# Wider warming, a new load order, and GpSimd's and VectorE's setup work reordered in a kernel of 16 conditioned tiles

## The reference

```python
x = x + einsum('bct,bcd->bdt', x, W0[cond])          # W0: 16 x 32 x 32
base  = einsum('bsi,oi->bso', x, W)                  # W: 512 x 512
low   = einsum('bsi,bir->bsr', x, A[label])          # A: 5 x 512 x 32
delta = einsum('bsr,or->bso', low, Bw) * 0.5         # Bw: 512 x 32
x = x + base + delta
```

## Time and profile before

| | us |
|---|---|
| median of 3 runs | 88.79 |
| lowest, highest | 87.93, 89.1 |
| the profiled execution | 88.51 |
| its span (first to last instruction) | 86.7 |
| TensorE busy in it | 82.6 |
| VectorE, ScalarE, GpSimd busy | 55.8, 39.6, 23.3 |

### The profile page before, as it was taken

One profiled execution on the slowest core, in us unless ns is written; L12 is line 12 of the kernel. 1 busy time (PEld: TensorE's weight loads), 2 busy tenths in 40 slices (PEclk: granted clock), 3 DMA queues, 4 the chain that ended last, 5 costly groups with the idle time before them and its releaser, 6 DMA issues.

```text
span 86.7 us, 1411 instructions
## 1 busy us (share of the span) xinstructions
PE 82.6 (95%) x463; PEld 72.9 (84%) x463; DVE 55.8 (64%) x117; ACT 39.6 (46%) x80; POOL 23.3 (27%) x37
## 2 busy tenths in 40 slices
PE   5999999999999999999999999999999999999950
PEld 5999999998888988898889888988898888889940
DVE  3672879975984696469744984499249933731550
ACT  0544492233547573457255616551754273415440
POOL 5322798977008001800170008000710000000000
PEclk9999999999999999999999999999999999999999
DMA  1999990370000494646037502770250015000606
GB/s 27 314 350 310 199 188 19 83 178 12 8 0 8 147 267 81 203 126 176 2 140 230 134 0 83 230 186 0 80 177 0 0 50 192 8 0 3 239 14 228
DMA packets 12393, 10.16 MB, mean 117 GB/s; under 512 B 1508, under 2 KB 9572, under 8 KB 12388
## 3 DMA queue, kind: packets, MB, share of 16 engines
q1 hardware_dynamic: 11444, 9.24, 38.1%
q10 hardware_dynamic: 432, 0.59, 2.1%
q0 software_dynamic: 512, 0.26, 1.7%
HBM read 5.90 MB, written 4.19 MB: 116 GB/s over the span
## 4 chain that ended last, share of the span: by engine, by line
PE 95%; DVE 1%; issue 0%
PE p_u L588 15%; PE p_u L589 15%; PE p_u L590 15%; PE p_low L573 5%; PE p_low L578 5%; PE p_low L574 4%; PE p_low L639 4%; PE p_u L599 4%; PE p_y L605 4%; PE p_y L606 4%; PE p_y L608 4%; PE p_u L616 3%; PE p_y L588 2%; PE p_y L589 2%; PE p_y L590 2%; PE p_y L643 2%
## 5 line engine op out<-in xcount | busy, mean ns | idle before, releaser
L252 POOL DMA_INDIRECT w_sel<-in_L_cond_weights,w_row x16 | 16.3, 1019 | 33.4 <-DVE diag L499 30.3
L588 PE MATMUL p_u<-m_hi,xt_hi 128*128 128x512 f32 (+1 forms) x60 | 22.6, 377 | 0.0
L589 PE MATMUL p_u<-m_lo,xt_hi 128*128 128x512 f32 (+1 forms) x60 | 22.6, 377 | 0.0
L590 PE MATMUL p_u<-m_hi,xt_lo 128*128 128x512 f32 (+1 forms) x60 | 22.5, 375 | 0.0
L410 DVE TENSOR_TENSOR xt_lo<-xt,xt_hi 128x512 fp32r<-128x512 f32 x14 | 10.1, 728 | 8.4 <-ACT xt_hi L308 8.4
L396 DVE STREAM_TRANSPOSE xt<-x_sb 128x512 f32<-128x512 f32 x14 | 15.1, 1091 | 0.0
L416 DVE TENSOR_TENSOR u_lo<-p_u,u_hi 128x512 fp32r<-128x512 f32 (+1 forms) x15 | 9.3, 652 | 8.9 <-ACT u_hi L313 8.8
L318 ACT ACTIVATE y_sb<-p_y 128x512 f32 (+1 forms) x13 | 7.7, 591 | 12.2 <-PE p_y L608 12.2
L590 PEld LDWEIGHTS p_u<-m_hi,xt_lo 128*128 128x128 f32 x60 | 11.3, 188 | 2.1
L588 PEld LDWEIGHTS p_u<-m_hi,xt_hi 128*128 128x128 f32 x60 | 11.3, 188 | 1.9
L589 PEld LDWEIGHTS p_u<-m_lo,xt_hi 128*128 128x128 f32 x60 | 11.3, 188 | 1.8
(11 more groups left out here) (92 smaller groups left out, 126.7 us busy)
## 6 DMA issues: line engine op xcount, KB each, us to landing
x_sb<-in_x SPq DMA_DIRECT2D x28, 128.0 KB
out<-y_sb SPq DMA_DIRECT2D x7, 512.0 KB, 3.2
w_sb<-in_L_cond_W ACTq DMA_DIRECT2D x2, 256.0 KB, 3.9
w_sb<-in_L_cond_W SPq DMA_DIRECT2D x2, 256.0 KB, 3.8
x_rows<-in_x SPq DMA_DIRECT2D x2, 256.0 KB, 4.5
out<-y_sb SPq DMA_DIRECT2D x2, 256.0 KB, 2.1
a_sb<-in_L_cond_lora_A SPq DMA_DIRECT2D x1, 256.0 KB, 5.3
w_sel<-in_L_cond_weights,w_row POOLq DMA_INDIRECT x16
```

The costliest lines, as they stand in the source:

```text
L252: nc.gpsimd.indirect_dma_start(out=w0_sel[:, t, :], out_offset=None, in_=W0_rows, in_offset=bass.IndirectOffsetOnAxis(ap=w0_row[:, t:t + 1 ...
L588: mm(to, xt_hi[:, slot, c, rows], m_hi[:, c, cols], start=(c == 0 and half != 1), stop=False)
L589: mm(to, xt_hi[:, slot, c, rows], m_lo[:, c, cols], start=False, stop=False)
L590: mm(to, xt_lo[:, slot, c, rows], m_hi[:, c, cols], start=False, stop=False)
```

## The change

- The warming becomes 6 fp32r products with 512 columns (the same 128 columns read four times) instead of 7 fp32 products with 128.
- SyncE loads x tile 0 right behind Bw, and then all four W tiles in the order of their use (1, 0, 3, 2). ScalarE loads A's part of label 0 and the ids.
- The ids are converted by GpSimd, after its identities and before its adds on W, instead of by VectorE. TensorE transposes x tile 0 and spreads the ids ahead of all W tiles.
- VectorE makes `fold_parts` and `fold_to` between the diagonals of W tiles 1 and 0, and splits x tile 0 as before the split of M.
- TensorE transposes x tile 1 ahead of `lora_half(1)`.
- GpSimd makes `ad_lo` ahead of the first two gathers. ScalarE and VectorE handle `kept` of the first pair ahead of its `diag`.

```diff
--- before.py
+++ after.py
@@ -45,7 +45,7 @@
     ROWS = 2 * P
-    WARM = 7
+    WARM = 6
     H = O // 2
...
@@ -72,7 +72,7 @@
 
-        warm = sb("warm", [P, P])
+        warm = sb("warm", [P, P], F32R)
         ident = sb("ident", [P, P])
...
@@ -199,11 +199,9 @@
             sp.dma_start(bw_sb[:], Bw.rearrange("(o p) r -> p o r", p=P)).then_inc(s_bw_in, 16)
-            sp.dma_start(w_sb[:, 0], W[0:P, :]).then_inc(s_w_in[0], 16)
             sp.dma_start(x_rows[:, 0], x_tile[0]).then_inc(s_rows_in[0], 16)
-            sp.dma_start(ids_i[:, 0], cond.unsqueeze(0)).then_inc(s_cond_in, 16)
-            sp.dma_start(ids_i[:, 1], label.unsqueeze(0)).then_inc(s_label_in, 16)
-            sp.dma_start(w_sb[:, 2], W[2 * P:3 * P, :]).then_inc(s_w_in[2], 16)
+            for o in W_ORDER:
+                sp.dma_start(w_sb[:, o], W[P * o:P * (o + 1), :]).then_inc(s_w_in[o], 16)
             sp.dma_start(x_rows[:, 1], x_tile[1]).then_inc(s_rows_in[1], 16)
...
@@ -242,6 +240,10 @@
 
+            pool.wait_ge(s_cond_in, 16)
+            pool.wait_ge(s_label_in, 16)
+            nc.gpsimd.tensor_copy(ids_r[:], ids_i[:]).then_inc(s_ids, 1)
+
             for o in W_ORDER[2:]:
...
@@ -276,13 +278,12 @@
                                     ALU.subtract).then_inc(s_adiff, 1)
+            pool.wait_ge(s_adiff, 1)
+            pool.wait_ge(s_adhi, 1)
+            nc.gpsimd.tensor_tensor(ad_lo[:], a_diff[:], ad_hi[:].bitcast(F32), ALU.subtract).then_inc(s_adlo, 1)
             pool.wait_ge(s_w0_row, BT)
...
             gather(1)
-
-            pool.wait_ge(s_adiff, 1)
-            pool.wait_ge(s_adhi, 1)
-            nc.gpsimd.tensor_tensor(ad_lo[:], a_diff[:], ad_hi[:].bitcast(F32), ALU.subtract).then_inc(s_adlo, 1)
 
...
@@ -293,8 +294,8 @@
             act.dma_start(a_sb[:, 0].rearrange("p c r -> p (c r)"), A_cols[:, 0]).then_inc(s_a0_in, 16)
-            act.dma_start(w_sb[:, 1], W[P:2 * P, :]).then_inc(s_w_in[1], 16)
-            act.dma_start(w_sb[:, 3], W[3 * P:4 * P, :]).then_inc(s_w_in[3], 16)
+            act.dma_start(ids_i[:, 0], cond.unsqueeze(0)).then_inc(s_cond_in, 16)
+            act.dma_start(ids_i[:, 1], label.unsqueeze(0)).then_inc(s_label_in, 16)
 
...
@@ -350,8 +351,8 @@
             split_x(3, 1, 1)
+            hi_kept(0)
             hi_diag(0, 0)
-            hi_kept(0)
             stack_low(0)
...
@@ -431,7 +432,7 @@
 
-            nc.vector.memset(warm[:], 1.0).then_inc(s_warm, 1)
+            nc.vector.memset(warm[:].bitcast(F32), 1.0).then_inc(s_warm, 1)
             for j in range(BT):
...
@@ -442,7 +443,7 @@
                                            ALU.add).then_inc(s_row_of, 1)
-            nc.vector.tensor_copy(ones_r[:], warm[0:1, :]).then_inc(s_ids, 1)
+            nc.vector.tensor_copy(ones_r[:], warm[0:1, :].bitcast(F32)).then_inc(s_ids, 1)
 
...
@@ -457,24 +458,25 @@
 
-            dve.wait_ge(s_pool, 3)
-            for o in W_ORDER[:2]:
+            def diag_w(k):
+
+                o = W_ORDER[k]
                 dve.wait_ge(s_w_in[o], 16)
...
 
+            dve.wait_ge(s_pool, 3)
+            diag_w(0)
             dve.wait_ge(s_pool, 4 + Q)
...
             nc.vector.tensor_copy(fold_to[:], fold_parts[:]).then_inc(s_group, 1)
-
-            dve.wait_ge(s_cond_in, 16)
-            dve.wait_ge(s_label_in, 16)
-            nc.vector.tensor_copy(ids_r[:], ids_i[:]).then_inc(s_ids, 1)
+            diag_w(1)
             dve.wait_ge(s_ids_all, 1)
             nc.vector.tensor_copy(ids_all[:].rearrange("p u b -> p (u b)"), p_fold[:, 0:2 * B]).then_inc(s_ids_sb, 1)
+            split_rows(0, p_low)
 
...
@@ -483,7 +485,6 @@
 
-            split_rows(0, p_low)
             split_m(0, 0)
...
@@ -511,10 +512,10 @@
             split_x(3, 1, 1)
-            spread(0, 0, used=1)
             dve.wait_ge(s_keep, 1)
...
             split_low(0)
+            spread(0, 0, used=1)
             split_diag(0, 0)
...
@@ -636,7 +637,7 @@
             for i in range(WARM):
-                mm(p_low[:, 0:P], warm[:], warm[:], start=True, stop=True)
+                mm(p_low[:], warm[:], warm[:].unsqueeze(1).broadcast_to([P, 4, P]), start=True, stop=True)
 
...
@@ -655,12 +656,12 @@
             transpose_groups(p_y[1], a_rep).then_inc(s_aT, 1)
+            transpose_rows(0, p_low)
+            spread_ids()
             pe.wait_ge(s_diag, 1)
...
             transpose_w(1)
-            transpose_rows(0, p_low)
-            spread_ids()
             pe.wait_ge(s_b_stack, 1)
...
@@ -668,9 +669,9 @@
             transpose_w(3)
-            lora_half(1)
             pe.wait_ge(s_ids_sb, 1)
             transpose_rows(1, p_fold)
+            lora_half(1)
 
...
             main_tile(p_y[0], 0, 0, left, half=0)
```

## The result

The changed kernel takes 89.23 us (median of 20 runs, 88.51 to 89.83), the kernel before 88.50 (20 runs, 87.93 to 89.1). The ratio is 1.0084, 95% interval 1.0057 to 1.0111: slower by 0.8%, where 0.8 us faster was forecast. The profiled execution took 89.68 us with a span of 87.9, against 88.51 and 86.7.

The account below looks back on a forecast made before the run. TensorE, busy 95% of the span, was taken to bound the kernel; gains could come only from the first 20 us. Waits of -0.67 and warming of -0.05 made -0.7 us: 87.8 or 88.1, called 88.0, range 87.0 to 89.2.

Parts of the forecast that it names:

- GpSimd reordered: `ad_lo` before the gathers: removes TensorE's waits of 0.19 us at `ad_lo` and 0.23 at `low_pair(1)`; later gathers stay covered.
- the worst bound: Gathers landing by 18.9 us, at most 2.4 after GpSimd's second; work ends at 21.8, second fold wants it at 22.4.
- The third rival: Waits only change their name: W0 or W2 late, or gathers holding VectorE; gives back 0.5 to 0.8 us, 88.7; chance 0.16.
- The loop and the tail: TensorE has no idle time there, 8.98 us per pair of tiles, so the change can't shorten them.
- The waits at tile 1, at `ad_lo` and at `low_pair(1)`: TensorE's excess of 0.25, 0.19 and 0.23 us at these places goes, 0.67 us in sum.
- The ids on GpSimd: GpSimd converts the ids at about 4 to 5 us, taking 0.4 to 1 us; nothing waits.
- The landings: First loads by sum of bytes: x tile 0 at 3.9 us, W1 4.7, W0 5.5, W3 6.3, W2 7.0, x tile 1 7.8.
- spare time for W0: W0's transfer and diagonal add have 1.4 us before TensorE needs them, so the load order costs nothing.
- The warming: Six wide products at the start: clock effect taken as 0, bounded by -1.0 and +2.8 us; at most 0.05 us gained otherwise.
- The later clock: Rival: TensorE's full clock comes later in the setup; 89.5 us, or 90.8 by the bound; chance 0.14.
- the hole: TensorE does nothing for about 0.35 us, from 3.65 to 4.0, between the warming and the first transposes.

Follow-up runs that it names:

- e3_load_held: The changed kernel, with SyncE issuing x of pair 3 only when gathers 0 and 1 have landed: six runs from 87.32 to 91.25 us, median 90.15.
- e7_adlo_between: The changed kernel, with GpSimd's order made gather 0, `ad_lo`, gather 1: 88.12 us, ratio 0.9946 to the kernel before.
- e2_gather_first: The changed kernel, with the first two gathers back ahead of `ad_lo` on GpSimd: 88.35 us, ratio 0.9977 to the kernel before.
- e10_no_gather_wait: The changed kernel, with pair 0's mix leaving out the rows of W0 and the wait for gathers 0 and 1: 87.26 us, ratio 0.9863.
- e6_two_queues: The changed kernel, with W tiles 1 and 3 on ScalarE's queue behind the ids, 0 and 2 on SyncE's: 89.59 us, ratio 1.0115.
- e5_adlo_first_only: The kernel before, with only `ad_lo` moved ahead of gathers 0 and 1 on GpSimd: 92.52 us, median of six.
- e4_wide_warm_only: The kernel before, with only the wide warming of 6 fp32r products of 512 columns: 88.34 us, ratio 0.9966.

## Why the prediction was wrong

**The step that failed** is the price of "GpSimd reordered": "with that bound they land by 18.9 ... Covered by 0.6 us at the worst bound". Mix ran at 20.20 instead of 18.9, 1.3 us later, and even 18.9 would have been too late. So two terms were too small and a deadline was missing.

- Issue: gather 1 was put at 15.5 to 16.5 and ran 16.11 to 17.50. The W tiles landed late (W2's add ended at 8.71 instead of 7.6), so `w_row`, `a_diff` and `ad_lo` were each 0.5 us or more behind my times, and the gather took 1.39 us on GpSimd instead of the 0.95 of the earlier trace rows. This is 1.0 of the 1.3 us.
- Flight: I took 2.4 us from the end of the gather to its use as an upper bound for any place. It came from a stretch in which no other load ran. The gather's new place lies beside x of pair 3, a load that SyncE issues when pair 1's x is transposed. It took 2.70 us there, and 1.57 in e3_load_held, where that load was held back. This is the other 0.3 us: the bound was loose for a quiet stretch, and a bound read from a quiet stretch is none for a busy one.
- The work behind mix was priced right: up to the end of `kept_lo` it took 2.83 us (2.9 forecast). TensorE wanted the second fold at 22.2 (22.4 forecast), so with mix at 20.20 it waited 0.9.
- Deadline: I followed the delay to the second fold and stopped. The stricter deadline was the low products of pair 2. They end a chain from mix over `kept` of pair 1, two transposes, `xt_lo`, two `u_lo` and the next pair's mix and `diag`, then ScalarE's `diag_hi` and `xt_hi`, to the `xt_lo` of tile 5. It took 8.88 us in e7_adlo_between (18.64 to 27.52) and 8.87 in the changed kernel. TensorE wanted its end 7.88 us after it began pair 1's first tile (19.94 to 27.82 before). So mix has to run some 1.1 us before that tile; with the forecast arrival of 19.24 that is about 18.2 us, and my own 18.9 was too late by 0.7. The runs agree: no wait with mix 1.3 or 1.5 us ahead (e2_gather_first, e10_no_gather_wait), 0.9 us with 0.2 ahead (e7_adlo_between).

One piece of that chain I left untested. Tile 5 is transposed by 25.01 us in the changed kernel, but ScalarE's `xt_hi` of it runs at 27.83, behind `diag_hi` of pair 1 in ScalarE's stream, and VectorE waits 1.00 us for it (1.01 before). Moving it ahead could loosen the deadline by up to that much, by this estimate; no run shows it.

The third rival named this place, "gathers that hold VectorE's queue ahead of `keep_low(1)`", but priced it at 0.5 to 0.8 us and gave it 0.16. It costs 2.0 us (e10_no_gather_wait).

**What was right.** The loop and the tail didn't change. The waits at tile 1, at `ad_lo` and at `low_pair(1)` are gone; TensorE reached pair 1's tiles 0.80 us early, for 0.7 forecast; without the gather's wait the kernel is 1.2 us faster, of which the 0.7 and the 0.3 of the warming make 1.0; the rest I can't assign. `xt_lo` beside a gather instead of `ad_lo` is fast again: two take 1.47 us together, where the first alone took 1.40; with `ad_lo` back beside them (e2_gather_first) two took 2.78. The ids on GpSimd took 0.45 us from 4.21 and held nobody.

**What was off without deciding.** The landings: by windows of before I had 313 and 336 GB/s, and it was 215 and 280. Of the 1.4 us of spare time for W0 0.2 us was left (its diagonal was added at 7.17; TensorE went on from W1 to W0 at about 7.4). The warming: 0 taken, -0.3 us measured. The later clock, my rival on the slower side, didn't happen: the transposes of x tile 0 are at the slow rate to 6.67 us (1.00 us for four) and W's at the fast one from 6.92, as forecast with 6.7, and the hole was 0.02 us between matmuls, not 0.35.

## What to carry to other kernels

When work is moved later on one queue, look up who waits for it in order, and follow that engine's queue to the next place where it has no spare time: the first deadline that you find need not be the strictest. A transfer's flight time holds only where nothing else is under way; ask which load will be issued in its new place. And between two orders that each stall, look for a piece that fits in the wait itself: gather 0 in GpSimd's wait for `ad_hi`, `kept` in VectorE's wait for `diag_hi` made the version with the lowest ratio of those that leave nothing out (0.9920).

## What the runs showed of the hardware

- A wait of TensorE costs more than itself when the clock falls behind it. After a wait of 2.1 us in the setup (1.9 between matmuls, e6_two_queues) the granted clock of the next 2 us was 0.53; after one of 2.8 (2.6 between matmuls, e5_adlo_first_only) it was 0.68 and 0.81 over the next 7. Behind the 1.4 us stall of the changed kernel (1.0 between matmuls) it stayed at 1.00.
- In the first microseconds the granted-clock line says 1.00 while a transpose takes 0.214 us instead of 0.12. The rate, not the line, shows where the clock rises, and that point moves by over a microsecond from one execution to the next of kernels with the same start: the four transposes of `a_rep`, begun between 4.7 and 4.9 us, took 1.06 us in the changed kernel and 0.60 in e2_gather_first.
- With the same order of loads the same 256 KB load of x tile 0 took 4.5 us to land in the kernel before and about 6 in one execution of e4_wide_warm_only, where TensorE waited 1.4 us for it.
- VectorE's subtractions are slower beside one on GpSimd: two `xt_lo` took 2.78 us together beside `ad_lo` (e2_gather_first) and 1.47 beside a gather (the changed kernel).
- A gather of 32 packets took 2.88 us from issue to use with the DMA engines free, and 3.28 to 4.09 beside a load of x, in one execution each.
